# Message products of a graph layer formed in place in PSUM, with their buffer released later

## The chip, the cores and the metric

One core of a Trainium2 chip (trn2) runs the kernel. Its engines work side by side: PE (TensorE, matrix products into PSUM), DVE (VectorE), ACT (ScalarE), POOL (GpSimd, which here issues the indirect DMAs) and SP (SyncE, which issues plain DMAs). They meet through semaphores. The metric is the device time of one execution in microseconds; lower is better.

## What is computed

Two graph layers over 6250 nodes with 16 features and 206250 edges, sorted by destination. The change is in the second. For each edge, two 16 x 16 matrices are made from its 16 attributes, one for messages, one for attention, each multiplied by the features of the edge's source node; a softmax over the edges of one destination, for each of the 256 places by itself, weighs the messages:

```
w_m = (efeat @ W_msg + b_msg).reshape(E, in_f, -1)
w_a = (efeat @ W_attn + b_attn).reshape(E, in_f, -1)
h_src = feat[src][:, :, None]
e1 = w_m * h_src
e2 = w_a * h_src
seg_max = jax.ops.segment_max(e2, dst, num_segments=N)
ex = jnp.exp(e2 - seg_max[dst])
denom = jax.ops.segment_sum(ex, dst, num_segments=N)
attn = ex / denom[dst]
ft = jax.ops.segment_sum(e1 * attn, dst, num_segments=N)
return ft.sum(axis=1)
```

## The kernel before

The second layer starts at about 3120 us of the span. Nodes are ranked by degree and laid 128 to a group, one node to a partition. A window (number k) is a group's next edges, at most 48 for each node, in `nh` half blocks of `HALF` = 3 edges; two halves make a block of `BLK` = 6 edges, `nb` = ceil(nh / 2). There are 50 windows, in a loop of 25 rounds over two parities `q`, each engine with its own copy of the loop. `nh` falls from 16 to 8 in their course (the second window alone has 6).

PE makes the weights of a half block, 3 matmuls of 256 columns, into one of the two halves of the PSUM buffer `psW` (`weights`, L546 to L550); the attention weights come first for all blocks of the window, then the message weights. In the first phase DVE multiplies each half by the rows of the source nodes in `gath` (`times_h`, L1162, called by `scores`), the result goes to `score` in SBUF, and a running maximum is kept. In the second, DVE takes the maximum from a block (`from_max`, L1192), ACT takes exponents in place in `score` (L703), and `messages` (L1197) forms the two half products of message weights and node rows in `prod`, a ring of `RING` = 3 blocks in the SBUF tile `stage`, then multiplies the block by the exponents (L1207). PE adds blocks up in `psS`: `prod_sums` (L562, line L565) those of `prod`, and `exp_sums` (L558, line L560) the exponents, in the next window's first phase.

Semaphores set the order: `w_ready` counts halves that PE has filled, `w_free` halves that DVE has read, `q_ready` finished blocks of `prod`, `q_free` blocks that PE has added. PE's message phase is one pass over b: message weights of block b+1, transposes of the next window's edge rows (L543), wait for `q_ready` of block b, its sums, and a closing matmul that releases the ring (L618). The first two halves of attention weights of the next window (`first_weights`, L553) come ahead of the last block's wait. PE's code for the two parities is long; the branch back to its start is L574.

POOL gathers the node rows of the next window by indirect DMAs, 3 to a half block (L350), in steps that `pace` (L425) ties to DVE's progress: half 6 waits for the first product of the running window, half 8 for the third. After the last gather POOL issues one transfer of the edges' attribute rows (L387) and the scatter of a finished group (L411). DVE's scores of a window wait until all its gathers have landed.

## Time and profile before

| | us |
|---|---|
| median of 3 runs | 6460.06 |
| lowest, highest | 6455.27, 6462.39 |
| the profiled execution | 6439.39 |
| its span | 6437.6 |
| second layer (from 3120 us on) | 3317 |

The rows come from the profiled execution. In the views by time, a row gives start, length, engine, line, operation, output and inputs, count, and in brackets the idle time of the engine ahead of it with what ended it. In the view by lines, a row gives count, busy time, mean of one in ns, and idle time ahead. DVEq, PEldq are the instruction queues' own steps (branches, register work) of an engine.

### The profile page before, as it was taken

To read this page: it belongs to the slowest core of one execution; us is meant where nothing else is said; L and a number is where in the kernel's file an instruction comes from. 1 tells how busy PE (TensorE), PEld (TensorE's weight loads), DVE (VectorE), ACT (ScalarE), POOL (GpSimd) and SP (SyncE) were. 2 spreads that over 40 slices of the span, in tenths; PEclk is the share of its full clock that TensorE was granted. 3 is DMA by queue.
4 is the path that set the end of the run, shared out by engine and by line. 5 is a ranking of instruction groups with operands and counts; after the bars stand their busy time and mean duration, and the time that the engine had idled before them with its cause. 6 is when DMAs were issued, how large, how long until landed. Compare 5 with 4: busy or idle time off the path is not lost.

```text
span 6437.6 us, 57655 instructions
## 1 busy us (share of the span) xinstructions
PE 2772.1 (43%) x13533; PEld 1969.5 (31%) x13534; DVE 3553.6 (55%) x4214; ACT 1210.3 (19%) x1559; POOL 3973.4 (62%) x3713
## 2 busy tenths in 40 slices
PE   3530000000000000000357778788787788778777
PEld 1110000000000000000245556556566566556555
DVE  8321112121222222233458888888888888878886
ACT  3430000000000000000122222222222322322222
POOL 0325766767767677665466666666666666666663
PEclk6555555555555555555678888888888888888888
DMA  5861111111111111111100111111111111111110
GB/s 160 265 213 19 20 26 26 27 26 27 27 28 32 26 33 30 32 37 30 20 13 20 21 29 21 21 21 29 21 21 29 29 21 29 26 24 29 29 29 19
DMA packets 158168, 255.12 MB, mean 40 GB/s; under 512 B 73726, under 2 KB 130563, under 8 KB 145156
## 3 DMA queue, kind: packets, MB, share of 16 engines
q0 software_dynamic: 126192, 100.10, 8.8%
q1 hardware_dynamic: 31711, 151.31, 7.1%
q8 instruction: 218, 3.57, 0.2%
q14 instruction: 15, 0.12, 0.0%
q10 hardware_dynamic: 32, 0.01, 0.0%
HBM read 113.57 MB, written 136.63 MB: 39 GB/s over the span
## 4 chain that ended last, share of the span: by engine, by line
issue 22%; PE 21%; DVEq 19%; DVE 14%; POOL 14%; DMA 6%; another core or an unknown queue 2%; ACT 1%; POOLq 1%; SPq 0%; ACTq 0%
POOL gath L350 12%; PE psS L560 8%; PE psS L565 6%; DVEq L1204 4%; PE psW L549 4%; DMA table<-arena 3%; DVE stage L1165 3%; DVEq L1172 2%; DVE stage L1207 2%; DVEq L1132 2%; DVE work L767 1%; DMA gath<-h_dram,hidx 1%; DVE arena L1165 1%; POOL info_dram L321 1%
## 5 line engine op out<-in xcount | busy, mean ns | idle before, releaser
L350 POOL DMA_INDIRECT gath<-h_dram,hidx x1695 | 1942.7, 1146 | 1105.1 <-issue 552.8
L350 POOL DMA_INDIRECT gath<-table,blkidx x1646 | 1613.1, 980 | 545.6 <-issue 509.8
L543 PE MATMUL psT<-identb,stage 128*100 128x128 bf16 x2448 | 208.2, 239 | 2497.5 <-issue 2474.0
L565 PE MATMUL psS<-stage,ident 128*128 128x256 f32 x3390 | 929.1, 430 | 142.6 <-DVE stage L1207 137.0
L543 PEld LDWEIGHTS psT<-identb,stage 128*100 128x100 bf16 x2448 | 191.4, 141 | 2523.7 <-issue 2489.8
L560 PE MATMUL psS<-arena,ident 128*128 128x256 f32 x3390 | 869.9, 401 | 0.5 <-issue 0.5
L1165 DVE TENSOR_TENSOR arena<-psW,gath 128x768 f32 (+1 forms) x565 | 521.9, 952 | 546.8 <-DMA gath<-h_dram,hidx 312.6
L565 PEld LDWEIGHTS psS<-stage,ident 128*128 128x128 f32 x3390 | 707.5, 216 | 294.7 <-DVE stage L1207 175.4
L549 PE MATMUL psW<-wst,stage 100*128 100x256 bf16 x3396 | 583.8, 296 | 403.1 <-DVE arena L1165 256.5
L560 PEld LDWEIGHTS psS<-arena,ident 128*128 128x128 f32 x3390 | 652.7, 204 | 89.2 <-issue 0.6
L703 ACT ACTIVATE arena<-arena 128x1536 f32<-128x1536 f32 (+1 forms) x294 | 421.4, 1433 | 993.7 <-DVE arena L1194 984.5
L1165 DVE TENSOR_TENSOR stage<-psW,gath 128x768 f32 (+1 forms) x565 | 514.4, 950 | 26.2 <-issue 14.8
L1207 DVE TENSOR_TENSOR stage<-stage,arena (+1 forms) x294 | 498.6, 1696 | 30.3 <-ACT arena L703 4.2
L549 PEld LDWEIGHTS psW<-wst,stage 100*128 100x128 bf16 x3396 | 298.6, 103 | 681.2 <-DVE arena L1165 285.3
L1194 DVE TENSOR_TENSOR arena<-arena,psT 128x1536 f32 (+2 forms) x294 | 495.4, 1685 | 0.0
L671 ACT ACTIVATE work<-work 128x48 f32<-128x48 f32 x50 | 12.1, 243 | 2241.2 <-DVE work L1017 1468.3
L700 ACT COPY stage<-psT 100x1024 bf16<-100x1024 bf16 x306 | 301.2, 997 | 86.8 <-remote 66.3
L1179 DVE TENSOR_TENSOR work<-work,arena 128x1536 f32<-128x1536 f32 x171 | 300.7, 1758 | 15.7
L722 ACT ACTIVATE work<-work 128x256 f32<-128x256 f32 x50 | 20.8, 416 | 1429.9 <-DVE work L1190 1429.9
L508 PE MATMUL psW<-stage,work 102*125 102x460 bf16 (+1 forms) x400 | 190.0, 614 | 179.8 <-ACT arena L654 148.1
L974 DVE SCALAR_TENSOR_TENSOR bstf<-tabs,info 128x1 f32 (+1 forms) x52 | 8.4, 161 | 396.0 <-issue 388.0
L598 PE MATMUL psS<-efraw,ident 128*128 128x512 f32 x100 | 103.0, 1133 | 273.1 <-DVEq L1134 257.1
(222 smaller groups left out, 2464.1 us busy)
## 6 DMA issues: line engine op xcount, KB each, us to landing
table<-arena SPq DMA_DIRECT2D x50, 1610.0 KB
ef<-arena SPq DMA_DIRECT2D x50, 805.7 KB
gath<-h_dram,hidx POOLq DMA_INDIRECT x1695
gath<-table,blkidx POOLq DMA_INDIRECT x1646
arena<-in_edge_attr SPq DMA_DIRECT2D x50, 257.8 KB
table<-arena SPq DMA_DIRECT2D x50, 186.9 KB
arena<-first_dram POOLq DMA_DIRECT2D x1, 915.5 KB, 13.7
info<-info_dram POOLq DMA_DIRECT2D x2, 432.0 KB, 6.5
```

What stands on the lines that cost most here:

```text
L350: pool.indirect_dma_start(out=gath[:, q, s, :], out_offset=None, in_=rows, in_offset=bass.IndirectOffsetOnAxis(ap=idx[:, q, s:s + 1].bitca ...
L543: last = nc.tensor.transpose(psTb[0:KE, t % 2, j, 0:GP], efs[:, 8 * t + j, :], identb[0:GP, 0:GP])
L549: last = nc.tensor.matmul(psW[0:GP, h % 2, j * IO:(j + 1) * IO], efT[:, q, h * HALF + j, 0:GP], wst[:, c0:c0 + IO], start=True, stop=True)
L560: nc.tensor.matmul(psS[0:GP, 0:IO], ident[0:GP, 0:GP], score[:, q, s, :], start=False, stop=False)
L565: nc.tensor.matmul(psS[0:GP, IO:2 * IO], ident[0:GP, 0:GP], prod[:, c0:c0 + IO], start=False, stop=False)
L700: nc.scalar.copy(efT[:, q, 8 * t:8 * t + 8, 0:GP], psTb[0:KE, t % 2, :, 0:GP]).then_inc(m["efT_sb"], 1)
L703: nc.scalar.activation(v, v, ACT.Exp).then_inc(m["exp_done"], 1)
L1165: V.tensor_tensor(dst_ap.rearrange("p s (i o) -> p s i o", o=D), psW[0:GP, s, 0:HALF * IO].rearrange("p (s i o) -> p s i o", i=D, o=D), bc ...
L1179: V.tensor_tensor(macc, macc, score[:, q, ds(b * BLK, BLK), :], ALU.max).then_inc(m["scored"], 1)
L1194: V.tensor_tensor(blk, blk, mnew.unsqueeze(1).to_broadcast([GP, n, IO]), ALU.subtract).then_inc(m["sub_done"], 1)
L1204: V.drain()
L1207: V.tensor_tensor(pr, pr, score[:, q, ds(b * BLK, n), :].rearrange("p s c -> p (s c)"), ALU.mult).then_inc(m["q_ready"], 1)
```

## The change

The two half products of a message block are written back to where the weights are, in `psW`, and not to `prod`. The full product then reads `psW` (both halves) and `score`, and writes `prod`. So a half of `psW` is no longer free when its half product is done, only when the block's full product is. Message halves no longer count `w_free`; PE waits for `q_ready` of the block before instead, which now starts at 1. The waits of POOL's `pace` and of PE's sums on `q_ready` are raised by that 1 and mean the same products as before. The wait for `q_free` moves from ahead of the half products to ahead of the full one.

```
@@ POOL, pace @@
                 elif b == 6:
-                    pool.wait_ge(m["q_ready"], done + 1)
+                    pool.wait_ge(m["q_ready"], done + 2)
                 elif b == 8:
-                    pool.wait_ge(m["q_ready"], done + 3)
+                    pool.wait_ge(m["q_ready"], done + 4)
@@ PE @@
-            def weights(c0, q, h, at0):
-                pe.wait_ge(m["w_free"], at0 + (h + 1))
+            def weights(c0, q, h):
                 for j in range(HALF):
...
-            def first_weights(w, q, at0):
+            def first_weights(w, q, done):
                 pe.wait_ge(m["efT_sb"], w * (S // 8) + 3)
+                pe.wait_ge(m["q_ready"], done + 1)
                 for h in range(2):
-                    weights(0, q, h, at0)
+                    weights(0, q, h)
+
+            def score_weights(q, h, tb):
+                pe.wait_ge(m["w_free"], tb * 2 + (h + 1))
+                weights(0, q, h)
+
+            def message_weights(q, h, tb, nb):
+                if h < 2:
+                    pe.wait_ge(m["w_free"], tb * 2 + nb * 2 + (h + 1))
+                else:
+                    pe.wait_ge(m["q_ready"], tb + (h // 2 + 1))
+                weights(IO, q, h)
...
-                            pe.wait_ge(m["q_ready"], tb + (b + 1))
+                            pe.wait_ge(m["q_ready"], tb + (b + 2))
                             prod_sums(2 * b)
@@ DVE @@
-            for name, n in (("tbl_sb", 2), ("l0_math", 2), ("h_free", 2), ("efT_sb", 2), ("w_free", 2), ("q_free", RING)):
+            for name, n in (("tbl_sb", 2), ("l0_math", 2), ("h_free", 2), ("efT_sb", 2), ("w_free", 2), ("q_ready", 1), ("q_free", RING)):
...
                     def messages(b, halves=2):
                         n = halves * HALF
+                        for s in range(halves):
+                            dve.wait_ge(m["w_ready"], th * 2 + nh + b * 2 + (s + 1))
+                            V.tensor_tensor(half(s), half(s), h_rows(b, s), ALU.mult)
+                        V.drain()
                         dve.wait_ge(m["q_free"], tb + b + 1)
+                        dve.wait_ge(m["exp_done"], tb + b + 1)
                         par = (b % RING) * (BLK * IO)
-                        for s in range(halves):
-                            times_h(prod[:, ds(par + HALF * s * IO, HALF * IO)].rearrange("p (s c) -> p s c", c=IO), b, s,
-                                    th * 2 + nh + b * 2, 3 - halves)
-                        V.drain()
-                        dve.wait_ge(m["exp_done"], tb + b + 1)
-                        pr = prod[:, ds(par, n * IO)]
-                        V.tensor_tensor(pr, pr, score[:, q, ds(b * BLK, n), :].rearrange("p s c -> p (s c)"),
+                        V.tensor_tensor(prod[:, ds(par, n * IO)].rearrange("p (s c) -> p s c", s=halves), psW[0:GP, 0:halves, 0:HALF * IO],
+                                        score[:, q, ds(b * BLK, n), :].rearrange("p (a s) c -> p a (s c)", a=halves),
                                         ALU.mult).then_inc(m["q_ready"], 1)
```

On DVE, a full message block in the loop of the first parity stands so before (ISA and REGISTER_ALU are register instructions, drains are not listed; the drain is ahead of the last row):

```order
L1194 TENSOR_TENSOR arena<-arena,psT 128x1536
L1199 ISA
L1163 ISA [waits s_q_free]
L1165 ISA [waits s_w_ready]
L1165 REGISTER_ALU
L1165 TENSOR_TENSOR stage<-psW,gath 128x768
L1163 REGISTER_ALU
L1165 ISA [waits s_w_ready]
L1165 REGISTER_ALU
L1165 TENSOR_TENSOR stage<-psW,gath 128x768
L1207 TENSOR_TENSOR stage<-stage,arena 128x1536 [waits s_exp_done]
```

and so now (the drain is behind the second product of 128x768):

```order
L1206 TENSOR_TENSOR arena<-arena,psT 128x1536
L1212 ISA
L1213 ISA [waits s_w_ready]
L1213 TENSOR_TENSOR psW<-psW,gath 128x768
L1212 REGISTER_ALU
L1213 ISA [waits s_w_ready]
L1213 TENSOR_TENSOR psW<-psW,gath 128x768
L1215 ISA
L1218 ISA [waits s_exp_done,s_q_free]
L1218 TENSOR_TENSOR stage<-psW,arena 128x1536
```

The register work of the ring's place and the wait for it have moved from ahead of the half products to behind the drain.

On PE, the first block of a window's message phase, from the matmul that carries the old sums over (L598) to the first block's sums, stands so before:

```order
L598 MATMUL psS<-efraw,ident 128x512 [waits s_sum_read]
L547 REGISTER_ALU
L549 MATMUL psW<-wst,stage 128x256 [waits s_w_free]
L549 MATMUL psW<-wst,stage 128x256 x2
...
L541 REGISTER_ALU
L543 MATMUL psT<-identb,stage 100x128 [waits s_efT_sb]
L543 MATMUL psT<-identb,stage 100x128 x7
L614 REGISTER_ALU
L565 MATMUL psS<-stage,ident 128x256 [waits s_q_ready]
```

and so now:

```order
L609 MATMUL psS<-efraw,ident 128x512 [waits s_sum_read]
L566 REGISTER_ALU
L548 MATMUL psW<-wst,stage 128x256 [waits s_q_ready]
L548 MATMUL psW<-wst,stage 128x256 x2
...
L541 REGISTER_ALU
L543 MATMUL psT<-identb,stage 100x128 [waits s_efT_sb]
L543 MATMUL psT<-identb,stage 100x128 x7
L576 MATMUL psS<-stage,ident 128x256 [waits s_q_ready]
```

Nothing has changed places; the second block's weights now wait for the same product as the first block's sums.

## Rows read from the trace of the kernel before

**Rows 1.** The page, part 1: busy time, share of the span, instructions.

```profile
PE 2772.1 (43%) x13533; PEld 1969.5 (31%) x13534; DVE 3553.6 (55%) x4214; ACT 1210.3 (19%) x1559; POOL 3973.4 (62%) x3713
```

**Rows 2.** Who waited for whom: total us, times, longest us.

```profile
DVE arena L1165 <- DMA gath<-h_dram,hidx: 312.6, 32, 122.9
```

**Rows 3.** DVE by line and shape, second layer: count, busy us, mean ns, idle before.

```profile
L1194 DVE TENSOR_TENSOR arena<-arena,psT 128x1536 f32 x221 | 386.2, 1748 | 0.0
...
L1207 DVE TENSOR_TENSOR stage<-stage,arena 128x1536 f32<-128x1536 f32 x50 | 87.9, 1758 | 4.9
...
L1194 DVE TENSOR_TENSOR arena<-arena,psT 128x768 f32 x23 | 21.8, 948 | 0.0
L767 DVE TENSOR_TENSOR psT<-work 128x256 f32<-128x256 f32 x50 | 21.7, 434 | 3.7
L1186 DVE TENSOR_TENSOR work<-work 128x256 f32<-128x256 f32 x50 | 21.3, 426 | 3.7
```

**Rows 4.** DVE in order of time, just ahead of a window's first message block.

```profile
5053.57 0.23 DVE L1137 SCALAR_TENSOR_TENSOR orow<-ft,info,xnew 128x16 f32<-128x16 f32 x1 [0.31 <-issue]
...
5054.41 0.27 DVE L1112 SCALAR_TENSOR_TENSOR hidx<-iotaf,erem,blkidx 128x48 int32<-128x48 f32 x1 [0.55 <-issue]
5054.98 0.96 DVE L1165 TENSOR_TENSOR stage<-psW,gath 128x768 f32<-128x768 f32 x1 [0.30 <-issue]
```

**Rows 5.** PE in order of time: a window's first message block; then one in full course.

```profile
5055.99 1.69 PE L549 MATMUL psW<-wst,stage 100*128 100x256 bf16 x6 [1.27 <-DVE stage L1165]
...
5058.71 3.66 PE L565 MATMUL psS<-stage,ident 128*128 128x256 f32 x12 [0.18 <-issue]
...
5004.17 0.83 PE L549 MATMUL psW<-wst,stage 100*128 100x256 bf16 x6
...
5005.86 2.86 PE L565 MATMUL psS<-stage,ident 128*128 128x256 f32 x12 [0.41 <-DVE stage L1207]
```

**Rows 6.** POOL, then DVE, around the end of an odd window of 14 half blocks.

```profile
3515.00 0.94 POOL L350 DMA_INDIRECT gath<-h_dram,hidx  x1 [2.72 <-DVE stage L1207]
...
3518.74 1.54 POOL L350 DMA_INDIRECT gath<-h_dram,hidx  x1 [0.30 <-issue]
...
3533.57 2.45 POOL L350 DMA_INDIRECT gath<-h_dram,hidx  x1 [0.30 <-issue]
...
3541.33 0.94 POOL L350 DMA_INDIRECT gath<-h_dram,hidx  x1 [0.30 <-issue]
...
3533.45 1.76 DVE L1207 TENSOR_TENSOR stage<-stage,arena  x1
3544.57 1.82 DVE L1165 TENSOR_TENSOR arena<-psW,gath 128x768 f32<-128x768 f32 x2 [9.36 <-DMA gath<-h_dram,hidx]
...
3549.64 0.96 DVE L1165 TENSOR_TENSOR arena<-psW,gath 128x768 f32<-128x768 f32 x1 [2.13 <-PE psW L549]
```

**Rows 7.** DVE at the start of an odd window that waits for no gather.

```profile
5573.00 1.82 DVE L1165 TENSOR_TENSOR arena<-psW,gath 128x768 f32<-128x768 f32 x2 [0.91 <-issue]
...
5579.00 0.96 DVE L1165 TENSOR_TENSOR arena<-psW,gath 128x768 f32<-128x768 f32 x1 [0.67 <-PE psW L549]
```

**Rows 8.** Two even windows' starts on DVE and POOL; last, line L574's own rows.

```profile
4763.72 1.82 DVE L1165 TENSOR_TENSOR arena<-psW,gath 128x768 f32<-128x768 f32 x2 [5.66 <-DMA gath<-h_dram,hidx]
...
4768.80 0.96 DVE L1165 TENSOR_TENSOR arena<-psW,gath 128x768 f32<-128x768 f32 x1 [2.13 <-issue]
...
4761.68 0.94 POOL L387 DMA_INDIRECT stage<-ef,ebst  x1 [0.30 <-issue]
...
4895.91 1.82 DVE L1165 TENSOR_TENSOR arena<-psW,gath 128x768 f32<-128x768 f32 x2 [1.31 <-PE psW L549]
...
4907.20 0.96 DVE L1165 TENSOR_TENSOR arena<-psW,gath 128x768 f32<-128x768 f32 x1 [2.00 <-PE psW L549]
...
4892.98 2.44 POOL L387 DMA_INDIRECT stage<-ef,ebst  x1 [0.30 <-issue]
...
L574 PEldq COMPARE_BRANCH  x25: 78/3990/6808, 3267.0 to 6412.6; - x25
```

More of the change, by code:

```diff
@@ L583, in _ @@
                         if h < MINH:
-                            weights(0, q, h, tb * 4)
+                            score_weights(q, h, tb)
                         elif h < NHW:
                             with pe.If(nh > h):
-                                weights(0, q, h, tb * 4)
+                                score_weights(q, h, tb)
                         with pe.If(prev > h - 2):
@@ L592, in _ @@
                     for h in range(2):
-                        weights(IO, q, h, tb * 4 + nb * 2)
+                        message_weights(q, h, tb, nb)
                     pe.wait_ge(m["valid_in"], k + 2)
@@ L601, in _ @@
                             if h < MINH:
-                                weights(IO, q, h, tb * 4 + nb * 2)
+                                message_weights(q, h, tb, nb)
                             else:
                                 with pe.If(nh > h):
-                                    weights(IO, q, h, tb * 4 + nb * 2)
+                                    message_weights(q, h, tb, nb)
                         if b + 2 < S // 8:
```

18 lines of the change are left out of this document (9 added, 9 removed).

## Prediction

> **What bounds the kernel now.** I read the page first, then the waits, then the stage from 3120 us on, window by window. The page says that no engine is full: POOL is busy 62% of the span, DVE 55%, PE 43% [rows 1]. The table of waits says where DVE, which carries each window from end to end, stands still: 312.6 us in 32 waits for the gathers of node rows, one of them 122.9 us long at the start [rows 2]. Inside a window DVE hardly pauses: products with the exponents of 1758 ns, subtractions of the maximum of 1748 ns [rows 3], half products of 0.95 us [rows 4]. A full message block is 1.76 + 1.75 + 2 x 0.95 = 5.41 us, less some 0.16 by which neighbours overlap, 5.25 us from product to product, and DVE is its limit. So DVE bounds the message part, and between two windows it is the later of POOL's gathers and PE.
>
> I call E the end of a window's last product, and count from it to the fourth score product of the next window; from there on DVE runs by itself. Windows alternate: the odd ones (second half of the loop's body) start without a loop branch on PE, the even ones after it.
>
> **Part 1: register instructions behind the drain.** The order of DVE's instructions shows two register instructions (L1215, L1218) that now stand between the drain behind the two half products and the full product; before, all the register work stood ahead of the first half product, where the 1.75 us subtraction hides it. The engine has nothing to run behind a drain, so they are in the open. What such a pair costs: the instruction of L1137 stands behind a drain and two register instructions and starts after 0.31 us of idle time, and the first half product of L1165, behind a drain and two more, after 0.30 [rows 4]; the product of L1207, with none in between, has 4.9 us ahead of it in 50 blocks, 0.10 each [rows 3]. So a pair costs 0.20 or a little more. There are two semaphores to wait for as well, where before one stood at the product. I take 0.30 for a block in the loop. Low end 0.20 (one of them overlaps the drain), high end 0.45 (0.55, the gap of L1112 behind a drain, a branch and two waits [rows 4], less 0.10). Blocks: 221 full ones in the loop (L1194, x221), 50 first ones (L1207, x50) with one plain register instruction and the second wait, 0.2 each, and 23 half ones at a window's end (L1194, x23), 0.2 each [rows 3]. Sum: 221 x 0.30 + 50 x 0.2 + 23 x 0.2 = 81 us, between 55 and 115.
>
> **Part 2: the instructions themselves.** The product now reads PSUM and SBUF: the subtraction, which does, takes 1748 ns against 1758 for two SBUF inputs, so 0 to -3 us over 271 full products. The half products now write PSUM: the one instruction that does this today takes 434 ns against 426 of its like in SBUF, 8 ns, 2 x 271 + 23 = 565 of them, 5 us [rows 3]. Together +3 us (-3 to +10). No row shows an instruction that reads and writes the same PSUM bank; that is a rival below. The Trainium skill ("Perfetto Trace Analysis", Optimizing Scalar/DVE Operations) speaks against the change here: a VectorE access costs about 125 ns at PSUM and 60 at SBUF, by which the 294 products would lose 19 us. The trace does not agree (1748 against 1758), and I go by the trace.
>
> **Part 3: weights later on PE.** The buffer comes free with the full product, 1.8 us later than with the half products. In the steady state this is hidden: PE's round of weights, transposes, sums and closing runs from 5004.17 to the sums' end at 5008.72, 4.55, less 0.41 of waiting, plus some 0.15 for the closing, about 4.3 us [rows 5] against DVE's 5.25, and the weights of the first half are ready about 0.6 us after the product, while the subtraction covers 1.6. It is not hidden at the first block of a window. There PE comes from a wait; its clock is at 1.2 GHz (weights 1.69, sums 3.66 instead of 0.83 and 2.86 [rows 5]). Today the second block's weights and the transposes are done before the first product ends; now all of it follows: 1.3 + 0.9 + 3.7 to 4.5 + 0.5, then 0.5 for the next half's weights, 6.9 to 7.7 us after the first product, and DVE wants them at 5.25 + 0.3 + 1.6 = 7.2. Late by 0 to 0.5, 0.3 taken, 50 windows: 15 us. If the clock rises only after the sums it is up to 1.2 each, 60 us; if as early as today, nothing. At E, where the last block is full, the next window's six first weights (0.7 us) now stand after the product and ahead of the last sums; DVE's own gap of 0.91 there [rows 7] covers their first half, but everything later on PE moves by 0.7, by about 0.5 with a half block.
>
> **Part 4: POOL's gathers.** A gather issue takes 0.94 us, and some take 1.54 or 2.45: those that meet a product or another instruction with two SBUF inputs on DVE end 0.94 after it. In the window that ends at 3535.2, 18 gathers follow the third product, which paces them; four meet products, 0.6 + 3 x 1.5 = 5.1 us in excess, and all 18 go back to back. DVE then waits 9.36 us [rows 6]. No issue is prolonged by the subtraction or a half product, which read PSUM and SBUF. So with the new operands 5.1 us go, and that wait falls to 4.3. The Trainium skill ("SBUF — State Buffer", Who interferes with whom; 🔬 SBUF: two separate sides) has the same as a lock: an instruction of VectorE with two SBUF inputs shuts out GpSimd on a shared port. By that rule, too, the trace agrees.
>
> What is late next is PE. Odd windows: the fourth score product comes 14.4 us after E now, of which the gathers hold 9.4 and a cold PE the rest [rows 6]. A window that doesn't wait for gathers has it at 6.9 [rows 7], now 7.6 with the 0.7 of part 3, or less with fewer skipped blocks. So the three largest odd windows win about 7 to 8 us, the next three (13 half blocks) 6, the five of 12 half blocks, 10.8 today, 3 (one of them 1): 55 us. From 11 half blocks on nothing is won, and the last eight lose 0.7 each: +5.
>
> Even windows: PE must first come through the branch at the loop's end (L574), median 3.99 us, up to 6.81 [rows 8]. The row gather of the edges (L387, the largest transfer of the stage) decides which. Issued 3.6 us after E, the fourth score product comes 10.7 after E; issued 1.6 before E, it comes at 12.6, although DVE's scores start 1.3 after E there and not 5.7 [rows 8]: the branch's code is fetched while the transfer is under way. Gathers that end 2.5 to 5 us earlier put L387 into that place in nearly all windows. So only the largest even window wins (4 us); a window of 12 or 11 half blocks loses 1.9 by the fetch and 0.5 by part 3, less 0 to 1: over the 15 even windows that wait for gathers today +18 us (between -10 and +30).
>
> Sum of part 4: -55 + 5 + 18 = -32 us (-70 to -5).
>
> **Sum.** 81 + 3 + 15 - 32 = +67 us. The profiled execution took 6439.4 us (span 6437.6), 0.3% under the median of the three runs, 6460.06. The terms are differences within that execution; put on the median they give 6527 us, 1.0% slower.
>
> **Rivals.**
> (a) The gathers pay in full, 12%. All issues prolonged by a product after the third one go, by the pattern of [rows 6] (5.1 us in the largest windows, 3.6 at 12 half blocks, 2.5 at 11) about 117 us, and PE is not in the way, because the fetch at L574 stays at its 4 us. For it: DVE's largest wait is this one. Against it: the 12.6 against 10.7 of [rows 8]. With 110 us won and the registers at their low end, 55 + 3 + 15 - 110 = -37, 6423 us. It decides as soon as the gathers bring more than parts 1 to 3 cost, about 99 us by my values, 73 with the registers at the low end.
> (b) The register pair and the cold PE at their high ends, 10%: 115 + 10 + 45 - 20 = +150, 6610 us.
> (c) The full product still shuts POOL out, because it still has an SBUF input beside a PSUM one, 8%: 81 + 3 + 15, and 0.6 on PE in some 30 windows, 18: +117, 6577 us. Against it: the subtraction has just these operands and prolongs nothing.
> (d) A half product that reads and writes the same PSUM bank runs at half speed, 3%: 565 x 0.95 = +537, about 7060 us. Nothing speaks for it but that no row shows it.
> (e) The forecast, 67%: 6527 us, its own range 6470 to 6580.
>
> **How the numbers follow.** A measurement of this kernel can tell about 0.2%, 13 us, from no change. Faster is (a), 0.12. Within 0.2% is the low end of the forecast together with part of (a)'s ground, registers at 55 and gathers at -60, 0.08. Slower is the rest, 0.80. The range reaches from between (a) and the forecast, 6450, to (b)'s edge, 6600; outside are most of (a), (d) and half of (b).
>
> **What would show it.** Part 1: DVE idle ahead of the full product, 0.10 us a block now, 0.3 to 0.5 after, and as many register rows behind each drain. Part 2: 1748 ns for the product, 950 to 960 for the half products. Part 3: waits of the first message half product for PE's weights, at the second block of a window alone. Part 4: no gather issue longer than 0.94 us beside a product; DVE's wait for gathers from 312.6 to under 200 us; instead waits for PE's weights at the second pair of scores, longest in even windows, with L574 nearer to 6 than to 4 us. The forecast is wrong if the gap ahead of the product stays under 0.2 us, or if L574 keeps its 4 us.

## The result and the profile after

The changed kernel takes 6773.8 us (median of 4 runs, 6761.8 to 6778.0), beside 6457.7 us of the kernel before in the same comparison: a ratio of 1.049, with a 95% interval of 1.0469 to 1.051. The prediction was 6527 us with a range of 6450 to 6600: the direction is right, the size is not. 67 us of loss were forecast, 316 came.

The profiled execution has a span of 6776.2 us. From the page of the profile after, the gathers and VectorE's rows of the second layer (columns as in [rows 3]: count, busy, mean ns of one, idle time ahead and what ended most of it):

```profile
L350 POOL DMA_INDIRECT gath<-h_dram,hidx x1695 | 1760.8, 1039 | 1495.8 <-issue 605.5
...
L1182 DVE TENSOR_TENSOR arena<-psW,gath 128x768 f32 (+1 forms) x565 | 519.9, 952 | 452.3 <-PE psW L548 250.0
L1213 DVE TENSOR_TENSOR psW<-psW,gath 128x768 f32<-128x768 f32 x565 | 521.4, 961 | 355.3 <-remote 331.0
...
L1218 DVE TENSOR_TENSOR stage<-psW,arena 128x1536 f32 (+2 forms) x294 | 498.4, 1695 | 117.0 <-issue 100.2
...
L711 ACT COPY stage<-psT 100x1024 bf16<-100x1024 bf16 x306 | 303.5, 999 | 262.3 <-remote 213.8
```

The rows of the page before that answer to them and did not stand in front:

```profile
L350 POOL DMA_INDIRECT gath<-h_dram,hidx x1695 | 1942.7, 1146 | 1105.1 <-issue 552.8
...
L1165 DVE TENSOR_TENSOR arena<-psW,gath 128x768 f32 (+1 forms) x565 | 521.9, 952 | 546.8 <-DMA gath<-h_dram,hidx 312.6
...
L1165 DVE TENSOR_TENSOR stage<-psW,gath 128x768 f32 (+1 forms) x565 | 514.4, 950 | 26.2 <-issue 14.8
L1207 DVE TENSOR_TENSOR stage<-stage,arena (+1 forms) x294 | 498.6, 1696 | 30.3 <-ACT arena L703 4.2
```

Three of VectorE's idle columns tell nearly the whole difference. Ahead of the scores it falls from 546.8 to 452.3 us, since a gather now takes 1039 ns and not 1146. Ahead of the full product it rises from 30.3 to 117.0. Both were forecast. Ahead of the half products of the messages it rises from 26.2 to 355.3, ended by something that the profile can only call remote, and this was not. The sum is -94.5 + 86.7 + 329.1 = +321 us, of 339 between the two spans. (Not all of the 94.5 is the shorter gathers' doing: the stalls below stand ahead of a window's end and give its gathers time to land. A measure without them follows in the part on the prediction.)

These 329 us are stalls, one in nearly every window: stretches in which an engine starts nothing although its data are there. VectorE by time, while the next window's gathers (14 half blocks) are issued:

```profile
3467.60 1.74 DVE L1206 TENSOR_TENSOR arena<-arena,psT 128x1536 f32 x1
3469.26 2.01 DVE L1213 TENSOR_TENSOR psW<-psW,gath 128x768 f32<-128x768 f32 x2
3471.66 1.76 DVE L1218 TENSOR_TENSOR stage<-psW,arena 128x1536 f32 x1 [0.39 <-issue]
3473.34 1.74 DVE L1206 TENSOR_TENSOR arena<-arena,psT 128x1536 f32 x1
3491.69 1.83 DVE L1213 TENSOR_TENSOR psW<-psW,gath 128x768 f32<-128x768 f32 x2 [16.61 <-remote]
```

The 16.61 us are no wait for weights: TensorE had written them by 3474.3. It stalls as well. Its weight loads for the sums of one block, by time:

```profile
3475.39 0.19 PEld L576 LDWEIGHTS psS<-stage,ident 128*128 128x128 f32 x1
3475.90 0.19 PEld L576 LDWEIGHTS psS<-stage,ident 128*128 128x128 f32 x1 [0.32 <-issue]
3478.04 0.19 PEld L576 LDWEIGHTS psS<-stage,ident 128*128 128x128 f32 x1 [1.95 <-issue]
3480.13 0.29 PEld L576 LDWEIGHTS psS<-stage,ident 128*128 128x128 f32 x1 [1.91 <-issue]
3481.54 0.29 PEld L576 LDWEIGHTS psS<-stage,ident 128*128 128x128 f32 x1 [1.11 <-issue]
3482.95 0.29 PEld L576 LDWEIGHTS psS<-stage,ident 128*128 128x128 f32 x1 [1.12 <-issue]
```

And ScalarE's copy of the transposes:

```profile
3485.07 1.01 ACT L711 COPY stage<-psT 100x1024 bf16<-100x1024 bf16 x1 [8.46 <-issue]
```

Loads that wait for nothing and follow each other every 0.2 us just before (7 in 1.38 us) start 1.41 to 2.14 us apart from the second row on, two or three times about 0.70. Three engines are held at once. The fourth is not: POOL issues gathers all the while, 18 in a row at 1.25 us, unbroken in the message phase for the first time because no product shuts it out (first two and last two):

```profile
3462.92 0.94 POOL L350 DMA_INDIRECT gath<-h_dram,hidx  x1 [5.48 <-DVE stage L1218]
3464.17 0.94 POOL L350 DMA_INDIRECT gath<-h_dram,hidx  x1 [0.30 <-issue]
...
3482.92 0.95 POOL L350 DMA_INDIRECT gath<-h_dram,hidx  x1 [0.30 <-issue]
3484.17 0.95 POOL L350 DMA_INDIRECT gath<-h_dram,hidx  x1 [0.30 <-issue]
```

TensorE slows some 13 us after the row has begun and goes on when it ends; VectorE comes last. Where 14 or 15 half blocks are being gathered VectorE loses 16.5 to 20.8 us so (but for the first window of 15, gathered beside the small window), at 13 8.8 to 12.7, at 12 4.0 to 8.4 in all, at 11 some 2 or nothing; in most windows of 10 to 8, where 18 gathers follow each other earlier in the window, it is 3.3 to 6.4 again.

Late code is not what holds them. From 3465 to 3495 us one DMA queue alone moved anything, that of POOL's gathers and scatters (packets, MB, share); the queue for instructions moved nothing, not even when VectorE ran again:

```profile
q0 software_dynamic: 720, 1.38, 16.9%
```

### The profile page after: what moved, and what is told of

Same layout as the page of the kernel before. It is cut to its first block, busy times and chain, and to the rows that moved or that the text cites. A ratio compares the mean times of both kernels' runs of the same rounds, so it can differ in the third digit from the quotient of the medians.

```text
span 6776.2 us, 57477 instructions
## 1 busy us (share of the span) xinstructions
PE 2745.3 (41%) x13533; PEld 1986.0 (29%) x13534; DVE 3563.3 (53%) x4214; ACT 1214.8 (18%) x1559; POOL 3794.4 (56%) x3713
## 4 chain that ended last, share of the span: by engine, by line
issue 28%; DVEq 19%; PE 18%; DVE 16%; POOL 6%; another core or an unknown queue 6%; DMA 4%; ACT 2%; POOLq 0%; SPq 0%; ACTq 0%
PE psS L571 7%; POOL gath L350 5%; PE psW L548 5%; PE psS L576 4%; DVEq L1214 4%; DVE stage L1218 3%; DMA table<-arena 3%; DVE psW L1213 2%; DVE arena L1206 2%; DVEq L1184 2%; DVEq L1143 2%; DVE work L778 1%; DVEq L779 1%; POOL info_dram L321 1%
## 5 line engine op out<-in xcount | busy, mean ns | idle before, releaser
L350 POOL DMA_INDIRECT gath<-h_dram,hidx x1695 | 1760.8, 1039 | 1495.8 <-issue 605.5
L576 PE MATMUL psS<-stage,ident 128*128 128x256 f32 x3390 | 982.1, 443 | 98.7 <-issue 98.1
L548 PE MATMUL psW<-wst,stage 100*128 100x256 bf16 x3396 | 569.1, 297 | 789.0 <-DVE stage L1218 418.7
L571 PE MATMUL psS<-arena,ident 128*128 128x256 f32 x3390 | 829.0, 387 | 0.0
L576 PEld LDWEIGHTS psS<-stage,ident 128*128 128x128 f32 x3390 | 741.8, 227 | 237.5 <-issue 120.1
L1182 DVE TENSOR_TENSOR arena<-psW,gath 128x768 f32 (+1 forms) x565 | 519.9, 952 | 452.3 <-PE psW L548 250.0
L1213 DVE TENSOR_TENSOR psW<-psW,gath 128x768 f32<-128x768 f32 x565 | 521.4, 961 | 355.3 <-remote 331.0
L571 PEld LDWEIGHTS psS<-arena,ident 128*128 128x128 f32 x3390 | 623.9, 195 | 77.5
L548 PEld LDWEIGHTS psW<-wst,stage 100*128 100x128 bf16 x3396 | 314.5, 104 | 1062.1 <-DVE stage L1218 503.2
L1218 DVE TENSOR_TENSOR stage<-psW,arena 128x1536 f32 (+2 forms) x294 | 498.4, 1695 | 117.0 <-issue 100.2
L1191 DVE TENSOR_TENSOR work<-work,arena 128x1536 f32<-128x1536 f32 x171 | 300.7, 1759 | 15.7
L665 ACT COPY arena<-psW 125x920 f32<-125x920 f32 x200 | 180.6, 929 | 180.1 <-DMA table<-arena 134.8
## 6 DMA issues: line engine op xcount, KB each, us to landing
arena<-first_dram POOLq DMA_DIRECT2D x1, 915.5 KB, 12.9
```

What stands on the lines that cost most here:

```text
L350: pool.indirect_dma_start(out=gath[:, q, s, :], out_offset=None, in_=rows, in_offset=bass.IndirectOffsetOnAxis(ap=idx[:, q, s:s + 1].bitca ...
L548: last = nc.tensor.matmul(psW[0:GP, h % 2, j * IO:(j + 1) * IO], efT[:, q, h * HALF + j, 0:GP], wst[:, c0:c0 + IO], start=True, stop=True)
L571: nc.tensor.matmul(psS[0:GP, 0:IO], ident[0:GP, 0:GP], score[:, q, s, :], start=False, stop=False)
L576: nc.tensor.matmul(psS[0:GP, IO:2 * IO], ident[0:GP, 0:GP], prod[:, c0:c0 + IO], start=False, stop=False)
L1182: V.tensor_tensor(score[:, q, ds(b * BLK + HALF * s, HALF), :].rearrange("p s (i o) -> p s i o", o=D), half(s), h_rows(b, s), ALU.mult).th ...
L1191: V.tensor_tensor(macc, macc, score[:, q, ds(b * BLK, BLK), :], ALU.max).then_inc(m["scored"], 1)
```

## What the profile before had of this

The grid of 0.70 us is in the trace of the kernel before, in the first layer, which the prediction did not use. There POOL gathers at 1.25 us too, and VectorE's small instructions start on a grid of 1.40:

```profile
797.85 0.45 DVE L1027 RECIPROCAL work<-work 128x48 f32<-128x48 f32 x1 [1.21 <-issue]
799.25 0.21 DVE L767 TENSOR_TENSOR work<-work,valid 128x48 f32<-128x48 f32 x1 [0.95 <-issue]
800.65 0.20 DVE L763 TENSOR_REDUCE lsum<-work 128x1 f32<-128x48 f32 x1 [1.19 <-issue]
802.05 0.21 DVE L767 TENSOR_TENSOR work<-work 128x48 f32<-128x48 f32 x1 [1.20 <-issue]
```

In its second layer the products hold POOL up every 5.3 us, and the stalls all but stay away: 26.2 us of idle time ahead of the message halves, 14.8 of them plain gaps of 0.3 us.

## The experiments

Theory S at the start: unbroken gathers hold the queues of the other engines. Rivals: the buffer held longer does it (H), or the registers behind the drain (R). The eighteen kernels ran in six groups, each on another chip with its own runs of the kernel before (e1 to e4, e5 to e8, e9 to e12, e13 and e14, e15 and e16, e17 and e18). A table of all stands at the end of this section.

**Undoing one part at a time.** e1 keeps TensorE's order of the changed kernel, with VectorE's products as before:

```
-                            V.tensor_tensor(half(s), half(s), h_rows(b, s), ALU.mult)
+                            V.tensor_tensor(prod[:, ds(par + HALF * s * IO, HALF * IO)].rearrange("p (s i o) -> p s i o", i=D, o=D),
+                                            half(s), h_rows(b, s), ALU.mult)
...
+                        pr = prod[:, ds(par, n * IO)]
+                        V.tensor_tensor(pr, pr, score[:, q, ds(b * BLK, n), :].rearrange("p s c -> p (s c)"),
+                                        ALU.mult).then_inc(m["q_ready"], 1)
```

> The order of the changed kernel on PE (the weights of a message block wait for the full product of the block before), but VectorE's products as before: half products written to SBUF, full product of two SBUF inputs, no register instructions behind the drain. Theory S (the stall comes from POOL issuing gathers back to back once no product holds it up): no stall over 5 us inside the message phase, only part 3 is paid, +10 to +60 us, 6470 to 6520. Rival H (the stall comes from the buffer held longer: PE late, then everybody late): the stalls of 8 to 20 us are there and the kernel takes 6700 or more.

Measured: 1.0044 (1.003 to 1.0058), +28 us. Ahead of the message halves 31.8 us end in something remote, in 12 waits of at most 4.3 us: small stalls, all in windows of 10 half blocks and fewer, but none of the long ones. So the hold alone doesn't make these, and H falls.

e2 puts register work and a second wait behind the drain of the kernel before:

```
                        V.drain()
+                        dve.wait_ge(m["q_free"], tb + b + 1)
                        dve.wait_ge(m["exp_done"], tb + b + 1)
+                        par = (b % RING) * (BLK * IO)
```

> The kernel before with the register work for the ring's place and the wait for it done a second time behind the drain, ahead of the full product. Part 1 of the prediction alone: gap ahead of the full product of 0.4 us instead of 0.10 in 221 blocks, +55 to +115 us, 6515 to 6575. If these stand beside other work after all: 6460 to 6475. If register instructions in the open are what opens the way to the stalls (rival R): stalls of 8 to 20 us, 6700 or more.

Measured: 0.9993 (0.9982 to 1.0003). No stalls, so R falls as far as this kernel goes. But it is a weak copy of part 1: the place was already in a register, and only 0.07 us a block came to stand ahead of the product (51.3 us in its page where the kernel before has 30.3). These 21 us cost nothing that can be measured.

**Breaking the gathers up.** e3 lets POOL wait for the landing of its last gather ahead of half blocks 10, 12 and 14:

```
+                            if b in (10, 12, 14):
+                                pool.wait_ge(hgath[q], (got0 + b) * (16 * HALF))
...
```

> The changed kernel, but POOL waits ahead of half blocks 10, 12 and 14 of the gathers until the gather issued last has landed, so that no more than 6 follow each other without a break of about 2 us. Theory S: no stall over 5 us in the message phase; POOL ends 2 to 6 us later in large windows, so part of it comes back as waits for gathers; 6450 to 6560. Rival H or R (hold, register instructions): the stalls stay, 6750 to 6800. If it is the number of gathers in a window and not their lack of breaks: stalls of the same length, only later.

Measured: 1.0276 (1.0259 to 1.0294). Ahead of the message halves the idle time falls from 355.3 to 114.5 us, the longest wait from 20.8 to 6.4. Windows of 11 and more half blocks, where the breaks stand, have no stall of 2 us in the message phase any more; what is left is in the smaller ones, ahead of half block 10, where up to 18 gathers still follow each other. But ahead of the scores idle time rises from 452.3 to 568.6. Waits for gathers account for 86 us of that (152.0 to 238.3); another 102.7 us, in 30 waits, end in something remote there, where the changed kernel has 12.6. Some look like stalls: at 3469.62, 4255.26 and 4753.03 VectorE starts its scores 8.5 to 8.9 us after the issue of the last gather that they need, where 2.4 is usual, while POOL goes on at 1.25 us. So e3 may in part have moved the stalls to the window's start. The time is above what I expected.

**Starting the gathers earlier.** e4 moves POOL's pacing waits by two half blocks:

```
-                elif b == 4:
+                elif b == 6:
                     pool.wait_ge(m["d_ready"], k)
-                elif b == 6:
+                elif b == 8:
...
-                elif b == 8:
+                elif b == 10:
...
```

> The changed kernel with each pacing wait of POOL moved two half blocks on (maximum ahead of half block 6, first product ahead of 8, third product ahead of 10): gathers start earlier and the last unbroken row has up to 18 gathers instead of 24. Theory S, with a stall that begins about 12 us into an unbroken row and ends with it: stalls of 16 to 20 us shrink to about 8 to 12, those of 12.5 to about 5, those of 5 to 8 go; 6500 to 6620. Rival H or R: no change, 6740 to 6790.

Measured: 1.0665 (1.0647 to 1.0682). This miss teaches: I had counted only the gathers behind the last pacing wait. In the large windows the stalls did shrink, from 16.5 or more to 10 to 15 us together. But the earlier start lets POOL run through 28 issues (27 gathers) without a longer pause, and so windows of 12 to 10 half blocks, which had lost 8 us or less, now lose 9 to 12. Ahead of the message halves it is 489.2 us in all, with no single stall over 12.0.

**Another chip, another picture.** The next four ran on another chip.

e5 moves the register work and the wait for the ring ahead of the half products again:

```
+                        dve.wait_ge(m["q_free"], tb + b + 1)
+                        par = dve.snap((b % RING) * (BLK * IO))
                        for s in range(halves):
...
                        V.drain()
-                        dve.wait_ge(m["q_free"], tb + b + 1)
                        dve.wait_ge(m["exp_done"], tb + b + 1)
-                        par = (b % RING) * (BLK * IO)
```

> The changed kernel with the register work of the ring's place and the wait for it moved ahead of the half products; behind the drain only the wait for the exponents stands. If part 1 is paid one for one: the gap ahead of the full product falls from 0.40 to 0.10 to 0.17 us in 221 blocks and the kernel gains 50 to 70 us, 6700 to 6725; the stalls stay. If the stalls hang on register instructions behind the drain: 6500. If the gap was covered by other waits (as e2 makes one think, where 0.07 us a block cost nothing): no change, 6760 to 6780.

e6 and e7 fill POOL's time with a memset of 0.45 us and a drain, ahead of each gather (e6) or after each third (e7), from half block 8 on. The edit of e7, behind the three gathers of a half block:

```
+                            if b >= 8:
+                                pool.memset(nrm[:], 0.0)
+                                pool.drain()
```

> The changed kernel, with a small memset of POOL and its drain ahead of each gather from half block 8 on: no waiting for a landing, only more time from one issue to the next (1.25 us now, some 1.7 to 2.0 then). Theory S as a matter of rate (the other engines are held once gathers have come every 1.25 us for some 12 us): no stall over 5 us in the message phase, waits for gathers return at the window's start, 6530 to 6680. If only a landed, empty queue helps, as in e3: stalls of 10 us and more stay, 6750 or more.

> The changed kernel, with one such memset and drain after every three gathers from half block 8 on: mean distance of the issues 1.25 to about 1.45 us. Theory S as a matter of rate, with a threshold between the 1.25 of the changed kernel and the 1.6 to 1.8 us of the kernel before (products holding POOL): stalls shorter than now, total between e6 and the changed kernel, 6560 to 6700. If any break resets it: no stalls at all and less waiting for gathers than e6, 6480 to 6560. If breaks without a landing don't help: 6770.

e8 is e4's edit on the kernel before:

> The kernel before with POOL's pacing waits two half blocks on, as in e4. There the same edit cost 113 us. Theory S: here the full products of two SBUF inputs hold POOL up every 5.3 us, so no stalls arise; gathers end some 5 to 10 us earlier, and of the 217 us that the first score product of a window waits today 80 to 150 go: 6320 to 6420. Rival: an earlier start alone brings the stalls, whatever holds POOL between: 6500 or more. Rival: windows' ends wait for PE and the branch instead: 6430 to 6460.

Measured: e5 0.9988 (0.9978 to 0.9997), e6 1.1429, e7 1.0358, e8 0.990 (0.9884 to 0.9917). All my numbers for e5 to e7 assumed stalls, and there are none, in e5 either, which has the unbroken gathers of the changed kernel. The reason stands in the runs of the kernel before: it takes 6207.5 us here, and 6460 where e1 to e4 ran. I call the two kinds of chip slow and quick. (Theory C, in the expectations from e9 on, is S on the slow kind alone.) The sharpest row is that of a branch in POOL's queue in the first layer (x and then shortest, median and longest, in ns), of the kernel before on the slow kind and of e9, below, on the quick kind:

```profile
L373 POOLq COMPARE_BRANCH  x795: 7/34/708, 562.2 to 2923.7; - x199
```

```profile
L373 POOLq COMPARE_BRANCH  x795: 34/34/55, 563.4 to 2755.0; - x199
```

No branch takes 0.7 us on the quick kind, and the last starts 169 us earlier: two thirds of the 252 us by which the kernel before is quicker. TensorE's clock does not make the kinds: in each of the five groups with several runs of the kernel before some had a mean granted clock of 0.68 to 0.72 and others of 0.91 to 0.93, and their times agree within 0.5%. VectorE's waits in the first layer, in the same order:

```profile
DVE bstf L974 <- issue: 379.6, 47, 11.7
DVE valid L1009 <- issue: 324.4, 48, 11.2
```

```profile
DVE bstf L985 <- issue: 99.2, 52, 3.5
DVE valid L1020 <- issue: 70.1, 50, 1.7
```

(e6 and e7 also show that a memset and a drain cost more than I took: issues 3.1 us apart in e6, against the 1.7 to 2.0 expected.)

**The changed kernel on the quick kind.** e9 is the changed kernel itself, e10 repeats e5, e11 e8 and e12 e1. The chip was another one, again of the quick kind.

> The changed kernel itself, once more, since the chip of e5 to e8 turned out to be of another kind than the one of the result and of e1 to e4: the kernel before takes 6208 us there and not 6460, and the steps of the instruction queues of 0.7 us that fill the first layer's profile are missing. Theory C (the stalls are this slowing of the queues, which comes only on such a chip and only under unbroken gathers): where the kernel before takes about 6208, no stalls, 6230 to 6300, a ratio of 1.003 to 1.015, near what the prediction's terms give; where it takes about 6460, 6770 again. Rival: the stalls belong to the change with registers behind the drain (e5 took them away by moving these): then 1.04 or more on either kind.

> The kernel of e5 again. Theory C: where the kernel before takes about 6208, ratio 0.999 as before; where it takes about 6460, the stalls are there as in the changed kernel and only some 40 to 60 us less than 6774, 6700 to 6740. Rival (registers behind the drain make the stalls): 6450 to 6480 on either kind.

> The kernel of e8 again: the kernel before with POOL's pacing two half blocks earlier. Theory C: ratio 0.990 again where the kernel before takes about 6208. Where it takes about 6460, the gathers are held by the full products and the maxima, but less of the window is left free of them: stalls of 1.8 to 4 us near a row's end in some windows, ratio 0.985 to 1.01. Rival: stalls as in e4, ratio above 1.03.

> The kernel of e1 again: the weights' buffer held longer, products as before. Part 3 is PE's lateness at a window's first blocks, which doesn't hang on the kind of chip: ratio 1.002 to 1.006 on either. If part of the 1.0044 of e1 was the slowing of the queues (waits of 2 to 4 us at the end of unbroken rows of 22 gathers in the small windows): 0.999 to 1.002 where the kernel before takes about 6208.

Measured: e9 1.0019 (1.001 to 1.0029), e10 0.9976 (0.9964 to 0.9988), e11 0.9893 (0.9876 to 0.9909), e12 1.003 (1.0016 to 1.0044). So the change costs 12 us there and not 316. VectorE's three rows in e9:

```profile
L1182 DVE TENSOR_TENSOR arena<-psW,gath 128x768 f32 (+1 forms) x565 | 520.4, 952 | 443.4 <-PE psW L548 267.4
...
L1218 DVE TENSOR_TENSOR stage<-psW,arena 128x1536 f32 (+2 forms) x294 | 498.3, 1695 | 114.6 <-issue 99.9
L1213 DVE TENSOR_TENSOR psW<-psW,gath 128x768 f32<-128x768 f32 x565 | 516.7, 958 | 13.4 <-issue 10.0
```

Nearly everything is as in the changed kernel on the slow kind, but for the 355.3 us ahead of L1213, which are 13.4. VectorE runs without a stall through 20 issues of POOL in a row (3232.8 to 3257.5, the last 18 gathers for 14 half blocks again, and two transfers behind them):

```profile
3241.32 1.76 DVE L1218 TENSOR_TENSOR stage<-psW,arena 128x1536 f32 x1 [0.40 <-issue]
3242.99 1.75 DVE L1206 TENSOR_TENSOR arena<-arena,psT 128x1536 f32 x1
3244.66 1.82 DVE L1213 TENSOR_TENSOR psW<-psW,gath 128x768 f32<-128x768 f32 x2
3246.88 1.76 DVE L1218 TENSOR_TENSOR stage<-psW,arena 128x1536 f32 x1 [0.40 <-issue]
```

**Back on the slow kind.** e13 is the kernel before, e14 has both edits of e5 and e4.

> The kernel before, unchanged, for its profile on this chip. Theory C: where it takes about 6208 us, the first layer's gathers end some 170 us earlier than in the profile of before (2938 us), no step of 0.7 us repeats in the queues of POOL and VectorE there, and the second layer is 20 to 50 us shorter than its 3288 us; VectorE's waits at a window's first score product are still near 200 us, since the products hold POOL on either kind. Rival: the two kinds differ in clock or DMA and everything is shorter in proportion.

> The changed kernel with both edits: registers ahead of the half products (e5) and POOL's pacing two half blocks earlier (e8's, e4's). Where the kernel before takes about 6208: the pacing has only the 80 us of first-score waits left to shorten, and PE sets the window's start: 0.988 to 0.997; if the gains of e8 (0.99) and e5 (0.998) add up: 0.985 to 0.988. Where it takes about 6460: long rows of up to 28 gathers, stalls as in e4, ratio 1.05 to 1.07.

Measured: 6427 us for e13, the slow kind, with a profile like the one of before. e14 1.0634 (1.0615 to 1.0654), with 488.0 us ahead of the message halves: registers ahead of the drain, by which the gap behind it falls from 0.40 to 0.24 us, don't keep the stalls away. R falls for good.

> The kernel of e7 again: the changed kernel with a memset and drain of POOL after every three gathers from half block 8 on. Where the kernel before takes about 6208: 6430 again. Where it takes about 6430 to 6460, theory C as a matter of the gathers' rate: no stall over 5 us in the message phase, and only what e7 costs on the quick kind (waits of up to 13 us for later gathers, ratio 1.036) is paid: 6650 to 6700. If a break of about a microsecond doesn't help: stalls of 8 us and more and 6850 or above.

> The kernel of e8 again: the kernel before with the pacing two half blocks earlier. Where the kernel before takes about 6208: ratio 0.990 again. Where it takes about 6430 to 6460: the products of two SBUF inputs and the maxima still hold POOL, the issues stay 1.4 us or more apart in the mean, and at most short waits of 1.8 to 4 us arise: ratio 0.985 to 1.01. Rival (an earlier start alone brings the stalls, as in e4 and e14): above 1.03.

e15 took 6748.9 us (a single run; 6466.4 before), with 133.1 us ahead of the message halves instead of 355.3. In its large windows the breaks do away with the stalls: none over 2 us before 5182 us. POOL there:

```profile
3476.60 0.95 POOL L350 DMA_INDIRECT gath<-h_dram,hidx  x1 [3.29 <-issue]
3477.86 0.95 POOL L350 DMA_INDIRECT gath<-h_dram,hidx  x1 [0.31 <-issue]
3479.11 0.95 POOL L350 DMA_INDIRECT gath<-h_dram,hidx  x1 [0.30 <-issue]
3480.06 0.45 POOL L472 MEMSET nrm<- 128x400 f32 x1
3482.40 0.95 POOL L350 DMA_INDIRECT gath<-h_dram,hidx  x1 [1.89 <-issue]
```

Three gathers in 5.8 us, in other places up to 7.2, and VectorE goes through. What stalls remain are in the small windows, ahead of half block 8, where e15 has no breaks. But the later gathers cost more than the stalls did: 653.9 us of idle time ahead of the scores, as on the quick kind (649.3 in e7).

e16 went against my expectation: 1.0211 (1.0177 to 1.0244), where the same kernel gains 1.0% on the quick kind. It has the products of two SBUF inputs, and stalls all the same, without any part of the change: no longer hold, no registers behind the drain, no product written to PSUM. All that it shares with e4 is the earlier stream of gathers. VectorE in one of its windows:

```profile
3518.69 1.75 DVE L1194 TENSOR_TENSOR arena<-arena,psT 128x1536 f32 x1
3523.17 1.82 DVE L1165 TENSOR_TENSOR stage<-psW,gath 128x768 f32 x2 [2.73 <-remote]
3525.08 1.76 DVE L1207 TENSOR_TENSOR stage<-stage,arena  x1
3526.76 1.75 DVE L1194 TENSOR_TENSOR arena<-arena,psT 128x1536 f32 x1
3537.60 1.82 DVE L1165 TENSOR_TENSOR stage<-psW,gath 128x768 f32 x2 [9.10 <-remote]
```

POOL made 40 issues there in a row of 59.5 us, 39 of them gathers, 1.5 us each in the mean. So a product that prolongs one issue in four or five doesn't save the row: 1.25 us apart is too much after 12 us, 1.5 in the mean after some 38, and 1.9 to 2.4 with real breaks is not. (In e3 a break of 2.2 us after each 6 gathers was enough too, 9.4 us for the six.) Whether the mean decides or the pieces at 1.25 us between two products stays open.

e17 was to show the kernel before on the quick kind; the chip was a slow one.

> The kernel before, unchanged, for its profile. Where it takes about 6208 us: waits at the first score product of about 215 us as on the slow kind (the products' hold on POOL is the same), half products without waits, the gap ahead of the full product 0.10; then the changed kernel of e9 is +84 us by the gaps ahead of the product and about -105 us by these waits, and the rest of its +12 us must lie at the second pair of scores. Where it takes about 6460: as e13.

> The kernel of e5 and e10 again. Where the kernel before takes about 6208: 6195 to 6200. Where it takes about 6430 to 6460: stalls as in the changed kernel (303 us ahead of the first half product of a block, 35 of them over 2.5 us), the gap ahead of the full product 0.24 instead of 0.40, together 6710 to 6760. If registers behind the drain had a part in the stalls: below 6600.

Measured: e17 6429 us, as e13. e18 6741.8 us beside 6423.1 (single runs both), 1.05, so nothing gained against the 1.049 of the changed kernel: 46 us less ahead of the product, 22 more ahead of the message halves.

All kernels, with VectorE's idle time in us by their pages, ahead of the full product, of the message halves and of the scores:

| kernel | chip | ratio | product | halves | scores |
|---|---|---|---|---|---|
| before (its profile, e13, e17) | slow | 1 | 30.3, 30.5, 30.7 | 26.2, 24.8, 25.3 | 546.8, 541.3, 543.6 |
| changed | slow | 1.049 | 117.0 | 355.3 | 452.3 |
| e1 hold alone | slow | 1.0044 | 28.1 | 72.3 | 545.0 |
| e2 registers alone | slow | 0.9993 | 51.3 | 31.8 | 542.9 |
| e3 landing breaks | slow | 1.0276 | 114.5 | 114.5 | 568.6 |
| e4 changed, earlier pace | slow | 1.0665 | 114.4 | 489.2 | 428.1 |
| e14 the same, registers ahead | slow | 1.0634 | 71.1 | 488.0 | 429.5 |
| e15 break every 3 | slow | 1.044 | 114.5 | 133.1 | 653.9 |
| e16 before, earlier pace | slow | 1.0211 | 31.8 | 299.8 | 440.3 |
| e18 registers ahead | slow | 1.05 | 71.2 | 377.8 | 459.3 |
| e9 changed | quick | 1.0019 | 114.6 | 13.4 | 443.4 |
| e5, e10 registers ahead | quick | 0.9988, 0.9976 | 71.6 | 25.3, 21.9 | 461.7, 461.9 |
| e12 hold alone | quick | 1.003 | 28.1 | 29.7 | 510.1 |
| e8, e11 before, earlier pace | quick | 0.990, 0.9893 | 30.4 | 14.8 | 465.4, 458.2 |
| e7 break every 3 | quick | 1.0358 | 114.5 | 14.9 | 649.3 |
| e6 each gather spaced | quick | 1.1429 | 114.6 | 15.7 | 1315.0 |

## Why the prediction was right in direction and wrong in size

**What failed: part 4, by a term put at nothing.** Part 4 took 5.1 us off a large window's row of gathers, asked what they would then collide with, and named TensorE's start of a window and the fetch behind L574. What the closer issues do to the other engines while they are being issued it put at nothing, without a reason, and no rival had it. On this kind of chip that is the largest term: 329 us more of idle time ahead of the message halves. The time that the products took from POOL was also what kept its issues apart. Where the stalls don't come the ratio is 1.0019, which put on 6460 us is 6472, inside the range, though under the 6527.

**The direction is right mostly by luck.** Of the 316 us that came, some 12 are what the prediction's own parts leave, as the quick kind shows, where it forecast 67. A change of 12 us is less than the 13 that it set as the least it could tell from none. That the kernel came out clearly slower is owed to the stalls, which it did not foresee.

**Part 1, registers behind the drain: the gap right, its price too high.** The gap is 0.40 us where it was 0.10, the 0.30 that was taken, and the sum of idle time rises by 87 us (81 forecast). But moving 43 of these us away again (e9 to e10, 114.6 to 71.6) brought 25 us on the quick kind, and e2's 21 nothing. A part of the gap is given back where VectorE waits for something else anyway: e10 waits 18 us longer than e9 ahead of the scores, and 8 longer ahead of the message halves. The prediction put all of it on the path, at 81 us; that was too much, though what the whole gap costs no run shows by itself.

**Part 2, the instructions: right.** Full products 1695 ns in the mean, as before (1696). Half products that read and write the same PSUM bank 961 against 950 ns, 565 x 11 = 6 us, forecast 5. Rival (d) falls. The Trainium skill (Perfetto Trace Analysis, Optimizing Scalar/DVE Operations) gives VectorE some 60 ns of access overhead per instruction on SBUF and some 125 on PSUM. The estimate of 19 us lost, worked out from this figure, isn't borne out: 1695 ns against 1696.

**Part 3, weights later on TensorE: right.** Forecast 15 us (0 to 60); e12 measures 18 us on the quick kind, with 13.8 us of waits for TensorE ahead of the message halves, 19 of at most 1.2. e1 measures 28 on the slow one, where 31.8 us of small stalls stand ahead of the same products.

**Part 4, POOL: the lock right, its worth on the window's start too small.** No gather meets a product any more: 1760.8 us of issues instead of 1942.7. Rival (c), that a product with an SBUF input beside a PSUM one still shuts POOL out, falls; the Trainium skill's rule (SBUF — State Buffer, Who interferes with whom), that a VectorE instruction with two SBUF inputs contends with a GpSimd instruction that reads SBUF and one with a single SBUF input doesn't, holds here too. VectorE's idle time ahead of the scores fell by 94 us on the slow kind, and by 67 between e12 and e9 on the quick kind, which differ only in VectorE's message products and their register work. Forecast were 32. Waits for gathers, forecast to fall from 312.6 to under 200 us, in the changed kernel, e12 and e9 (total us, times, longest us, one wait of 123 at the stage's start in each):

```profile
DVE arena L1182 <- DMA gath<-h_dram,hidx: 152.0, 2, 123.2
DVE arena L1182 <- DMA gath<-h_dram,hidx: 332.9, 37, 122.9
DVE arena L1182 <- DMA gath<-h_dram,hidx: 172.2, 12, 122.9
```

As foreseen the idle time doesn't fall by all of these: ahead of the scores e9 has 267.4 us of waits for TensorE's weights, e12 173.8.

Measured as the prediction did it, from the end of a window's last product to the fourth score product of the next: the odd windows together take 207.7 us in e12 and 149.1 in e9, 59 less, where 50 less were forecast from the kernel before. The even ones take 306.2 and 303.7, 2.5 less, where 18 more were forecast. On the slow kind it is 58 less and 26 less, with the stalls helping the gathers. So the odd windows were right, and the term mis-sized is the one for even windows. Its loss is there in four windows of 12 half blocks (9.7 to 10.3 us in e12, 12.9 to 13.9 in e9), but other even windows, large and small, win more. Rival (a), by which the gathers pay in full (117 us), got about half of its size. The sign that was named, L574 near 6 us and not near 4, did not come clearly either. The line is L585 now; changed kernel, e12, e9 (shortest, median, longest, in ns):

```profile
L585 PEldq COMPARE_BRANCH  x25: 78/4400/5900, 3280.0 to 6751.2; - x25
L585 PEldq COMPARE_BRANCH  x25: 78/4497/6680, 3065.0 to 6194.1; - x25
L585 PEldq COMPARE_BRANCH  x25: 78/4905/7068, 3075.1 to 6199.9; - x25
```

The median rose from 3.99 us to 4.40 on the slow kind, and to 4.91 with the new products on the quick kind, 0.4 over e12: the direction forecast, a fraction of the size. That the large transfer of L387 is what prolongs it stays unproven; no run moved it by itself.

**The quick kind's sum.** With the hold already paid in e12, the products' new operands cost 87 ahead of the product, take 16 off the message halves (the gap behind the drain covers TensorE's lateness) and 67 off the scores: +4 us. The two profiled executions differ by +6 (6219.1 and 6224.9), but the medians by -7, since the one profiled of e12 was among its shortest and that of e9 among its longest. With the +18 of the hold the medians give +11, which is e9's +12. No profile of the kernel before came from this kind, so this balance starts from e12 and not from it, and 10 us are as fine as it gets.

## What to carry to other kernels

A lock between two engines can also be a brake: before you take it away, ask which rate the freed engine then reaches, and whether the trace shows anywhere what happens at that rate, even in another layer. Idle time that ends in nothing the profile knows, on several engines at once and on a grid, is no scheduling matter of one engine. And a gap added on the busiest engine is not lost in full while that engine still waits elsewhere.

No kernel here beats the one before on both kinds: the kernel before with earlier pacing gains 1.0% on the quick kind (e8, e11) and loses 2.1% on the slow one (e16).

## What the runs showed of the hardware

- Under POOL's stream of indirect DMA issues the other engines' queues can fall to a step every 0.70 us or a multiple. It came on four of the six chips of the experiments and in the runs of the result, and not on the other two; the kernel before takes 6423 to 6466 us there and 6208 to 6210 here. Whether it is a property of the chip or of something that ran beside it can't be told, for each chip came up once. The changed kernel's four runs lie within 0.3% of each other, so it is no matter of the one execution that is shown; whether the profiler has a part in it no run shows.
- It follows POOL's rate: issues 1.25 us apart for 12 us bring it, 1.5 us in the mean for some 38 does too, three in 5.8 to 7.2 us don't. Six in 9.4 us with their break (e3) don't in the message phase either. Few points between were seen, and the kernels that gave them differ in more than the rate. That six with a break, 1.57 us in the mean, stay free where 1.5 in the mean do not speaks for the pieces without a break, but is no proof.
- What exactly is held is open. The gathers themselves were issued on time, every 1.25 us, through the stall. VectorE stood some 6 us longer than TensorE and ScalarE, for weights that had been there for 17. In other windows it ran again 2.7 to 3.2 us after the last gather, once before L387 was issued, so it did not wait for that transfer. Whether instructions or semaphores come late, the profile doesn't show.
- A POOL memset of 128x400 takes 0.45 us, but with its drain the next gather starts 1.6 to 3.3 us after it.
